# First group of sequences: value products ahead of the scores, f1 bias products behind them

## The chip, the cores and the metric

The kernel runs on one core of one Trainium2 chip. The metric is the device time of the program in microseconds (us); what is reported is the median of repeated runs.

## The reference, cut to what matters

One transformer layer in two halves, on x of 8 sequences x 512 tokens x 256 features, all in float32:

```
x = x + attn_block(layernorm(x))
x = x + ffn_block(layernorm(x))

attn_block(x):
  xn = layernorm(x, ln1_w, ln1_b)
  Q = elu(xn q_w' + q_b) + 1      # 64 features
  K = elu(xn k_w' + k_b) + 1
  V = xn v_w' + v_b               # 256 features
  out_n = sum_{m<=n} (Q_n.K_m) V_m / (sum_{m<=n} Q_n.K_m + 1e-6)
  x = x + out o_w' + o_b
  h = gelu(layernorm(x, ln2_w, ln2_b) f1_w' + f1_b)    # 1024
  return x + h f2_w' + f2_b

ffn_block(x):
  h = layernorm(gelu(x ternary(W_fc)'), ln_w, ln_b)    # 1024
  return h ternary(W_proj)'
```

`ternary(W)` rounds W / mean(|W|) to -1, 0 or 1.

## The kernel before

One sequence is one group g, 0 to 7. A group has four token tiles of 128. Each engine (TensorE: PE and its weight load PEld; VectorE: DVE; ScalarE: ACT; GpSimd: POOL; the DMA queue: SP) runs a list of steps in the order written in its functions `first()` (group 0 and the start of group 1), `step(g)` and `last()`. Nothing else sets the order: every step waits on semaphores, and whatever stands behind a waiting step on its engine waits with it. In `step(g)` the attention work of group g + 1 is mixed into the feed-forward work of group g, so TensorE always has something to run. Group 0's attention has no such partner: it is the prologue.

A float32 product of full accuracy is made as three products of split operands (`split3`, L177 to L179): hi by hi, lo by hi, hi by lo. ACT writes the hi half of an operand out of PSUM, DVE the lo half.

PSUM has eight banks: `bank_f0`, `bank_f1` (f1 and fc), `bank_y0`, `bank_y1` (f2, transposes of h), `bank_p` (projection), `bank_a0`, `bank_a1`, and `bank_a2`, which is also called `bank_q`.

The steps of the prologue, in TensorE's order before:

- `qkb`, `wvo_mm`, `tu(0, 0)`, `tu(0, 1)`, `qk_mm(0)`: bias of q and k, the product of the value and output weights, the transposes of u, and the products for Q and K into `bank_q`.
- `bvo` (L210): four products of 256 columns for the bias row, into `bank_p`.
- `f1b` (L218): 16 float32 products of **one column** each for the bias of f1, into `bank_y0`; every one needs a full weight load. The trace shows each as two records, 32 in all. DVE's `f1_bias_add` reads them; the first reader of its result is `gelu(0, 0)`.
- `scores(0)` (L271, L272): Q by K, eight products of 128 columns into `bank_q` (diagonal tiles), then 384, 384, 128, 128 columns into `bank_a0`, and 256, 256 into `bank_a1`. It waits for `qk_lo`, the last step of a chain through DVE and ACT that begins with `qk_mm(0)`. The three parts are masked and split by `ad_mask`, `ad_hi`, `ad_lo`, `ae_hi`, `ae_lo`, `af_hi`, `af_lo`.
- `v_mm(0, 0)`, `v_mm(0, 1)` (L177 to L179): 24 products of 256 columns, the values, into `bank_a0` and `bank_a1`. Those banks hold scores until `ae_lo` and `af_lo` have read them, so the values wait for these. ACT's `v_hi` and DVE's `v_lo` split the values.
- `attend(0, 0)` to `attend(0, 3)` (L303, then L177 to L179): for each token tile one product with the eps row (33 rows of weights) and 3, 6, 9 and 12 split products of 258 columns; 34 products in all. DVE's `attn_out` divides and adds.
- `tz2(0, 0)`, `theta_sum`, `tz2(0, 1)`, `f1(0, 0)` and so on: transposes of z, the mean of |W|, and the feed-forward products.

On the DMA queue (SP) the load of the projection weights, `pj_raw`, stands behind two waits, and the loads of x for group 1 behind it:

```
            sp.wait_ge(s["wf1_lo"], 4)
            sp.wait_ge(s["f1b_done"], 1)
            sp.dma_start(pj_raw, pj_d).then_inc(s["pj_loaded"], 16)
            load_x(1)
```

ACT's `abs_part(2)` and `abs_part(3)` read `pj_raw`, and stand on ACT ahead of `z2_norm(0, 0)`.

Of the kernel before, what the change touches and what calls it, by code (L numbers as in the profile page):

```python
# [8 lines left out]
ACT = mybir.ActivationFunctionType  # L9
AXX = mybir.AxisListType.X  # L10

P = 128
# [7 lines left out]
def build(nc, x, wqk_d, wv_d, wo_d, f1_d, f2_d, fc_d, pj_d, vec_d, rows_d, out):  # L20
    G, N, D = x.shape
# [13 lines left out]
    with ExitStack() as ctx:  # L35
# [11 lines left out]
        def by_k(b):  # L47

            return b[:].rearrange("p (k n) -> p k n", k=KD)

        wqk = [sb("wqk_hi", [P, KD, P], F32R), sb("wqk_lo", [P, KD, P], F32R)]
        wvo = [sb("wvo_hi", [P, KD, D], F32R), sb("wvo_lo", [P, KD, D], F32R)]
# [121 lines left out]
        def _(pe):  # L174
            def split3(ps, w, r, start, stop, skip=False):

                pe.matmul(ps, w[0], r[0], start=start, stop=False, skip_group_check=skip)  # L177
                pe.matmul(ps, w[0], r[1], start=False, stop=False, skip_group_check=skip)  # L178
                return pe.matmul(ps, w[1], r[0], start=False, stop=stop, skip_group_check=skip)  # L179
# [9 lines left out]
            def qkb():  # L189
                pe.wait_ge(s["wqk_loaded"], 16)  # L190
                pe.wait_ge(s["vec_loaded"], 16)
                for k in range(KD):
                    mm = pe.matmul(bank_f[0][:, 0:1], wqk_raw[:, k, :], ln1b_c[:, k:k + 1],
                                   start=(k == 0), stop=(k == KD - 1))
                mm.then_inc(s["qkb_done"], 1)

            def wvo_mm():
                pe.wait_ge(s["wv_loaded"], 16)
                pe.wait_ge(s["wo_loaded"], 16)
                for c in range(KD):  # L200
                    for k in range(KD):
                        mm = pe.matmul(bank_y[1][:, c * D:(c + 1) * D], wv_raw[:, k, c * P:(c + 1) * P],
                                       wo_raw[:, k, :], start=(k == 0), stop=(k == KD - 1))
                mm.then_inc(s["wvo_done"], 1)
# [74 lines left out]
                block_of(bank_a[1][:, 0:2 * P], 1, 2 * P, N).then_inc(s["s_done"], 1)  # L279

            def v_mm(g, h):
                pe.wait_ge(s["ae_lo" if h == 0 else "af_lo"], g + 1)
                if g == 0:
                    pe.wait_ge(s["wvo_lo"], 2)
                for j in range(2):
                    t = 2 * h + j
                    for k in range(KD):
                        mm = split3(bank_a[h][:, j * D:(j + 1) * D], [r[:, k, t * P:(t + 1) * P] for r in uT],
                                    [w[:, k, :] for w in wvo], k == 0, k == KD - 1)
                mm.then_inc(s["v_done"], 1)  # L290

            def attend(g, t):

                pe.wait_ge(s["v_lo"], 2 * g + t // 2 + 1)
                if t == 0:
                    pe.wait_ge(s["ad_lo"], g + 1)
                    if g == 0:
                        pe.wait_ge(s["eps_ready"], 1)
                        pe.wait_ge(s["rows_w"], 7)
                if t == 3:  # L300
                    pe.wait_ge(s["xa_ready"], 4 * g + 1)
                b = (bank_q, bank_a[0], bank_a[1], bank_q)[t]
                pe.matmul(b[:, 0:VW], ones_row[:], eps_row[:], start=True, stop=False)  # L303
                for j in range(t + 1):
                    if j == t:
                        w = [a[:, t * P:(t + 1) * P] for a in ad]
                    elif j == 1:
                        w = [a[:, (t - 2) * P:(t - 1) * P] for a in af]
                    else:
                        c = t - 1 if j == 0 else 3  # L310
                        w = [a[:, c * P:(c + 1) * P] for a in ae]
                    mm = split3(b[:, 0:VW], w, [r[:, j, :] for r in v], False, j == t)
                mm.then_inc(s["av_done"], 1)
# [85 lines left out]

            def first():  # L400

                qkb(); wvo_mm(); tu(0, 0); tu(0, 1); qk_mm(0); bvo(); f1b(); scores(0); v_mm(0, 0); v_mm(0, 1)
                attend(0, 0); attend(0, 1); attend(0, 2); attend(0, 3); tz2(0, 0); theta_sum(); tz2(0, 1); f1(0, 0)
                f1(0, 1); f1(0, 2); f1(0, 3); f2(0, 0); f2(0, 1); f2(0, 2); tu(1, 0); tu(1, 1); f1(0, 4); cpj()
                qk_mm(1); f2(0, 3); f1(0, 5); spread(); f1(0, 6); f2(0, 4); f2(0, 5); f1(0, 7); scores(1); f2(0, 6)
                f2(0, 7); v_mm(1, 0); v_mm(1, 1); attend(1, 0); attend(1, 1); tz3(0, 0); attend(1, 2); fc(0, 0, 0)
                tz3(0, 1); attend(1, 3); fc(0, 0, 1); fc(0, 1, 0); fc(0, 1, 1); tr(0, 0, 0); fc(0, 2, 0)
                tr(0, 0, 1); fc(0, 2, 1); tr(0, 0, 2); fc(0, 3, 0); proj(0, 0, 0); tr(0, 0, 3); tz2(1, 0)
                fc(0, 3, 1); proj(0, 0, 1); tz2(1, 1); tr(0, 1, 0); proj(0, 0, 2); proj(0, 0, 3)
# [35 lines left out]
        def _(act):  # L445
# [106 lines left out]
            def v_hi(g, h):  # L552
                act.wait_ge(s["v_done"], 2 * g + h + 1)
                if g:
                    act.wait_ge(s["av_done"], 4 * g)
                act.activation(v[0][:, 2 * h:2 * h + 2, 0:D], by_k(bank_a[h]), ACT.Copy).then_inc(s["v_hi"], 1)  # L556

            def z2_norm(g, h):
                act.wait_ge(s["ln2_sh"], 2 * g + h + 1)
# [53 lines left out]
            def first():  # L613

                ln3_hi(); wqk_hi(); u_norm(0, 0); u_norm(0, 1); u_hi(0, 0); u_hi(0, 1); wvo_hi(); qk_exp(0)
                wf1_hi(0); qk_hi(0); wf1_hi(1); n1(0); ae_hi(0); af_hi(0); wf1_hi(2); wf1_hi(3); ad_hi(0)
                v_hi(0, 0); eps_split(); v_hi(0, 1); abs_part(0); abs_part(1); abs_part(2); abs_part(3)
                z2_norm(0, 0); z2_norm(0, 1); z2_hi(0, 0); z2_hi(0, 1); gelu(0, 0); gelu(0, 1); gelu(0, 2)
                u_norm(1, 0); gelu(0, 3); u_norm(1, 1); u_hi(1, 0); u_hi(1, 1); gelu(0, 4); rows(); n1(1); qk_exp(1)
                gelu(0, 5); qk_hi(1); spread_copy(); gelu(0, 6); gelu(0, 7); ae_hi(1); ad_hi(1); af_hi(1)  # L620
                v_hi(1, 0); v_hi(1, 1); z3_norm(0, 0); z3_hi(0, 0); z3_norm(0, 1); z3_hi(0, 1); gelu3(0, 0, 0)
                gelu3(0, 0, 1); gelu3(0, 1, 0); gelu3(0, 1, 1); g_hi(0, 0, 0); gelu3(0, 2, 0); g_hi(0, 0, 1)
                gelu3(0, 2, 1); z2_norm(1, 0); g_hi(0, 0, 2); gelu3(0, 3, 0); z2_norm(1, 1); z2_hi(1, 0)
                g_hi(0, 0, 3); z2_hi(1, 1); g_hi(0, 1, 0); u_norm(2, 0); gelu3(0, 3, 1)
# [31 lines left out]
        def _(dve):  # L656
# [134 lines left out]
            def lo_part(dst, b, hi, ready):  # L791
                dve.tensor_tensor(dst, b, hi.bitcast(F32), ALU.subtract).then_inc(s[ready], 1)  # L792
# [40 lines left out]

            def v_lo(g, h):
                dve.wait_ge(s["v_hi"], 2 * g + h + 1)
                lo_part(v[1][:, 2 * h:2 * h + 2, 0:D], by_k(bank_a[h]), v[0][:, 2 * h:2 * h + 2, 0:D], "v_lo")

            def attn_out(g, t):

# [81 lines left out]
            def first():  # L921

                consts(); ln1_stats(0); wqk_lo(); qk_bias_add(); ln1_shift(0); u_lo(0, 0); u_lo(0, 1); wide_cols()
                wvo_lo(); qk_max(0); bo_rows(); ln3_lo(); qk_sum(0); wf1_lo(0); qk_lo(0); wf1_lo(1); ad_mask(0)
                ae_lo(0); af_lo(0); f1_bias_add(); wf1_lo(2); wf1_lo(3); ad_lo(0); v_lo(0, 0); eps_lo(); v_lo(0, 1)
                attn_out(0, 0); ln2_stats(0, 0); attn_out(0, 1); ln2_stats(0, 1); attn_out(0, 2); ln2_var(0, 0)
                ln2_stats(0, 2); attn_out(0, 3); ln2_stats(0, 3); ln2_var(0, 1); ln2_shift(0, 0); ln2_shift(0, 1)
                threshold(); z2_lo(0, 0); z2_lo(0, 1); ln1_stats(1); ternary(0); ln1_shift(1); ternary(1)
                ternary(2); selectors(); ternary(3); u_lo(1, 0); u_lo(1, 1); qk_max(1); qk_sum(1); qk_lo(1)
                ad_mask(1); ad_lo(1); ae_lo(1); af_lo(1); y_sum(0, 0); ln3_stats(0, 0); y_sum(0, 1); v_lo(1, 0)  # L930
                ln3_shift(0, 0); ln3_stats(0, 1); v_lo(1, 1); ln3_shift(0, 1); z3_lo(0, 0); attn_out(1, 0)
                ln2_stats(1, 0); attn_out(1, 1); ln2_stats(1, 1); z3_lo(0, 1); ln2_var(1, 0); attn_out(1, 2)
                ln2_stats(1, 2); ln4_stats(0, 0); ln2_shift(1, 0); attn_out(1, 3); ln2_stats(1, 3); g_lo(0, 0, 0)
                ln2_var(1, 1); g_lo(0, 0, 1); ln2_shift(1, 1); ln1_stats(2); g_lo(0, 0, 2); z2_lo(1, 0)
                g_lo(0, 0, 3); z2_lo(1, 1); ln1_shift(2); ln4_stats(0, 1); ln4_var(0, 0); g_lo(0, 1, 0)
# [181 lines left out]
```

## Time and profile before

| | |
|---|---|
| median of 3 runs | 541.44 us (540.43 to 543.45) |
| the profiled execution's own time | 542.56 us |
| its span, first to last instruction | 540.7 us |
| TensorE busy | 516.9 us, 96% of the span |
| VectorE, ScalarE, GpSimd busy | 336.3, 290.0, 128.6 us |
| mean granted clock of TensorE | 0.952 of 2.4 GHz |
| TensorE idle between 40.84 and 48.30 us | all but three short pieces |

The profile gives times from the start of the span. "Granted clock" is 1.00 where TensorE ran at 2.4 GHz and 0.50 where it ran at 1.2 GHz. A timeline row gives the start, the length, the engine, the line, the operation, the tile written and the tiles read, the shape, a count, and in brackets how long the engine had been idle and what ended that. The lengths of successive products overlap, so the time that a product takes in a row of products is read from the distance of two starts.

### The profile page before, as it was taken

The page shows a single profiled execution, that of the slowest core. Times are in us where ns is not written, and L with a number is a line of the kernel's source. Part 1 is how long each engine was busy: PE and PEld are TensorE (multiplying, and loading weights), DVE is VectorE, ACT ScalarE, POOL GpSimd, SP SyncE. Part 2 cuts the span into 40 slices and gives each one's busy share as a digit, 9 for nine tenths or more (in the row PEclk, how much of TensorE's full clock was granted, in tenths as well). Part 3 has the DMA queues.
Part 4 walks back from the last instruction along what each step waited for, and adds up shares of the span by engine and source line. Part 5 has one row for each costly group of instructions (what it writes and reads, how often), then busy time and mean ns, then how long its engine had stood idle before and what let it go on. Part 6 is the DMA issues. An engine that isn't in the chain of part 4 may idle for free.

```text
span 540.7 us, 8083 instructions
## 1 busy us (share of the span) xinstructions
PE 516.9 (96%) x2802; PEld 437.4 (81%) x2802; DVE 336.3 (62%) x930; ACT 290.0 (54%) x543; POOL 128.6 (24%) x128
## 2 busy tenths in 40 slices
PE   4895999999999999999999999999999999999887
PEld 3774878888888878888789888888788888888766
DVE  2668526865578627865388636776288725692467
ACT  3564652776248634677158553577248653563063
POOL 3204103422044021511144021420244102340110
PEclk9777998999999989999899998999899998999989
DMA  7130000100010000100000000100001000000001
GB/s 282 59 118 1 1 0 1 39 21 1 1 60 2 19 1 19 41 21 0 1 31 30 21 0 1 59 21 1 0 21 39 22 1 0 21 0 21 0 21 39
DMA packets 10039, 14.02 MB, mean 26 GB/s; under 512 B 784, under 2 KB 9104, under 8 KB 9488
## 3 DMA queue, kind: packets, MB, share of 16 engines
q1 hardware_dynamic: 10000, 13.52, 7.1%
q8 instruction: 22, 0.36, 0.3%
q14 instruction: 17, 0.14, 0.1%
HBM read 9.32 MB, written 4.19 MB: 25 GB/s over the span
## 4 chain that ended last, share of the span: by engine, by line
PE 92%; DVE 4%; ACT 1%; issue 1%; DMA 1%; SPq 0%; POOL 0%; DVEq 0%; ACTq 0%; POOLq 0%
PE bank_y L345 22%; PE bank_f L364 11%; PE bank_p L394 10%; PE bank_f L177 6%; PE bank_f L179 6%; PE bank_f L178 6%; PE bank_a L177 5%; PE bank_y L378 5%; PE bank_a L179 4%; PE bank_a L178 4%; PE bank_a L272 3%; PE bank_a L271 3%; PE bank_a L185 3%; PE bank_a L303 2%; PE bank_f L185 1%
## 5 line engine op out<-in xcount | busy, mean ns | idle before, releaser
L345 PE MATMUL bank_y<-wf,hring 128*128 128x256 f32 x512 | 121.5, 398 | 0.0
L345 PEld LDWEIGHTS bank_y<-wf,hring 128*128 128x128 f32 x512 | 103.4, 202 | 16.7 <-issue 0.2
L1003 POOL TENSOR_TENSOR rs<-ve,neg_half 128x2 f32<-128x2 f32 x48 | 33.6, 700 | 252.7 <-DVE ve L765 252.6
L909 DVE SCALAR_TENSOR_TENSOR g_lo<-bank_y,vec,g_hi 128x256 fp32r<-128x256 f32 x128 | 55.7, 477 | 23.4 <-ACT g_hi L610 22.6
L394 PE MATMUL bank_p<-wpj_t,g_hi 128*128 128x256 f32 x256 | 64.4, 288 | 0.5 <-DVE g_lo L909 0.5
L610 ACT ACTIVATE g_hi<-bank_y,vec 128x256 fp32r<-128x256 f32 x128 | 53.3, 472 | 20.8 <-PE bank_y L378 20.7
L579 ACT ACTIVATE hring<-bank_f,f_bias 128x512 f32<-128x512 f32 x64 | 43.9, 687 | 37.1 <-PE bank_f L179 36.3
L394 PE MATMUL bank_p<-wpj_t,g_lo 128*128 128x256 f32 x256 | 62.0, 279 | 0.0
L177 PE MATMUL bank_f<-z2T_hi,wf_hi 128*128 128x512 f32 x128 | 54.9, 429 | 1.4 <-DVE z2T_lo L792 1.4
L364 PE MATMUL bank_f<-wfc_t,z3T_hi 128*128 128x512 f32 x128 | 54.2, 423 | 0.5 <-DVE z3T_lo L792 0.5
L179 PE MATMUL bank_f<-z2T_hi,wf_lo 128*128 128x512 f32 x128 | 52.7, 411 | 0.0
L178 PE MATMUL bank_f<-z2T_lo,wf_hi 128*128 128x512 f32 x128 | 52.5, 410 | 0.0
L601 ACT ACTIVATE h<-bank_f 128x512 f32<-128x512 f32 x64 | 38.0, 596 | 25.2 <-PE bank_f L364 23.7
L364 PE MATMUL bank_f<-wfc_t,z3T_lo 128*128 128x512 f32 x128 | 51.1, 400 | 0.0
L394 PEld LDWEIGHTS bank_p<-wpj_t,g_hi 128*128 128x128 f32 x256 | 48.1, 188 | 1.5 <-DVE g_lo L909 0.7
L1021 POOL TENSOR_TENSOR xa<-xa,bo_b 128x512 f32<-128x512 f32 x16 | 20.4, 1293 | 119.1 <-ACT xa L498 119.1
L394 PEld LDWEIGHTS bank_p<-wpj_t,g_lo 128*128 128x128 f32 x256 | 48.2, 188 | 0.5
L889 DVE BATCH_NORM_STATS2 bn<-h 128x6 f32<-128x512 f32 x64 | 41.7, 682 | 4.2 <-ACT h L601 4.0
L378 PE MATMUL bank_y<-ident,h 128*128 128x128 f32 x256 | 37.0, 272 | 0.0
L378 PEld LDWEIGHTS bank_y<-ident,h 128*128 128x128 f32 x256 | 30.5, 141 | 3.7
L556 ACT ACTIVATE v_hi<-bank_a 128x512 fp32r<-128x512 f32 x16 | 9.6, 600 | 42.4 <-PE bank_a L179 42.4
L498 ACT ACTIVATE z<-y,sh,rs 128x256 f32<-128x256 f32 x32 | 17.5, 594 | 26.4 <-DVE sh L770 26.4
(155 smaller groups left out, 1015.1 us busy)
## 6 DMA issues: line engine op xcount, KB each, us to landing
x_sb<-in_x SPq DMA_DIRECT2D x16, 256.0 KB, 2.8
out<-yc SPq DMA_DIRECT2D x16, 256.0 KB, 2.1
h<-in_f SPq DMA_DIRECT2D x1, 1024.0 KB, 7.8
wf<-in_f SPq DMA_DIRECT2D x1, 1024.0 KB, 9.7
h<-in_fc SPq DMA_DIRECT2D x1, 1024.0 KB, 11.7
h<-in_pj SPq DMA_DIRECT2D x1, 1024.0 KB, 4.8
hring<-in_wv SPq DMA_DIRECT2D x1, 256.0 KB, 3.9
hring<-in_wo SPq DMA_DIRECT2D x1, 256.0 KB, 4.8
```

The costliest lines, as they stand in the source:

```text
L177: pe.matmul(ps, w[0], r[0], start=start, stop=False, skip_group_check=skip)
L178: pe.matmul(ps, w[0], r[1], start=False, stop=False, skip_group_check=skip)
L179: return pe.matmul(ps, w[1], r[0], start=False, stop=stop, skip_group_check=skip)
L345: mm = pe.matmul(bank_y[t // 2][:, (t % 2) * D:(t % 2 + 1) * D], hring[:, (8 * g + k) % RH, t * P:(t + 1) * P], wf2[:, k, :], start=(k == ...
L364: mm = pe.matmul(bank_f[c][:], z3T[part][:, k, t * P:(t + 1) * P], wfc[:, k, c * 512:(c + 1) * 512], start=(k == 0 and part == 0), stop=(k ...
L378: mm = pe.transpose(bank_y[q % 2][:, (2 * i + t) * P:(2 * i + t + 1) * P], h3[:, 2 * h + t, m * P:(m + 1) * P], ident[:])
L394: mm = pe.matmul(bank_p[:, t * D:(t + 1) * D], gr[part][:, (8 * g + 4 * h + q) % RG, i, t * P:(t + 1) * P], wpj[:, m, :], start=(m == 0 an ...
L579: act.activation(hring[:, (8 * g + m) % RH, :], bank_f[m % 2][:], ACT.Gelu, bias=f1_bias[:, m:m + 1]).then_inc(s["h_ready"], 1)
L601: act.activation(h3[:, t, c * 512:(c + 1) * 512], bank_f[c][:], ACT.Gelu).then_inc(s["h3_ready"], 1)
L610: act.activation(gr[0][:, n % RG, i, :], bank_y[q % 2][:, i * D:(i + 1) * D], ACT.Copy, scale=ln3w_c[:, m:m + 1]).then_inc(s["g_hi"], 1)
L889: dve.bn_stats(bn[3][:, t, 6 * c:6 * c + 6], h3[:, t, c * 512:(c + 1) * 512]).then_inc(s["ln4_bn"], 1)
L909: dve.scalar_tensor_tensor(gr[1][:, n % RG, i, :], bank_y[q % 2][:, i * D:(i + 1) * D], ln3w_c[:, m:m + 1], gr[0][:, n % RG, i, :].bitcast ...
```

## The change

In the first group only, the value products go to `bank_f0` and `bank_f1`, which are free then, so they no longer wait for the split of the scores; they wait for `wvo_lo` and for `qk_bias_ready` (the one-column product in `bank_f0` has been read). On TensorE they stand ahead of `scores(0)`, and `f1b` stands behind it. The waits for `ae_lo` and `af_lo` go to `attend(0, 1)` and `attend(0, 2)`, which write the banks that held the scores. ACT and DVE get the steps in a matching order: `v_hi`, `v_lo` right behind the split of q and k, `eps_split` and `eps_lo` ahead of the scores' split, `f1_bias_add` last. No instruction is added or removed.

```diff
+        def v_bank(g, h):
+
+            return bank_a[h] if g else bank_f[h]
...
             def v_mm(g, h):
-                pe.wait_ge(s["ae_lo" if h == 0 else "af_lo"], g + 1)
-                if g == 0:
+                if g:
+                    pe.wait_ge(s["ae_lo" if h == 0 else "af_lo"], g + 1)
+                else:
                     pe.wait_ge(s["wvo_lo"], 2)
+                    pe.wait_ge(s["qk_bias_ready"], 1)
...
+                if g == 0 and t in (1, 2):
+                    pe.wait_ge(s[("ae_lo", "af_lo")[t - 1]], 1)
...
-                qkb(); wvo_mm(); tu(0, 0); tu(0, 1); qk_mm(0); bvo(); f1b(); scores(0); v_mm(0, 0); v_mm(0, 1)
+                qkb(); wvo_mm(); tu(0, 0); tu(0, 1); qk_mm(0); bvo(); v_mm(0, 0); v_mm(0, 1); scores(0); f1b()
...
-                wf1_hi(0); qk_hi(0); wf1_hi(1); n1(0); ae_hi(0); af_hi(0); wf1_hi(2); wf1_hi(3); ad_hi(0)
-                v_hi(0, 0); eps_split(); v_hi(0, 1); abs_part(0); abs_part(1); abs_part(2); abs_part(3)
+                wf1_hi(0); qk_hi(0); v_hi(0, 0); v_hi(0, 1); n1(0); eps_split(); wf1_hi(1); ad_hi(0)
+                ae_hi(0); af_hi(0); wf1_hi(2); wf1_hi(3); abs_part(0); abs_part(1); abs_part(2); abs_part(3)
...
-                wvo_lo(); qk_max(0); bo_rows(); ln3_lo(); qk_sum(0); wf1_lo(0); qk_lo(0); wf1_lo(1); ad_mask(0)
-                ae_lo(0); af_lo(0); f1_bias_add(); wf1_lo(2); wf1_lo(3); ad_lo(0); v_lo(0, 0); eps_lo(); v_lo(0, 1)
+                wvo_lo(); qk_max(0); bo_rows(); ln3_lo(); qk_sum(0); wf1_lo(0); qk_lo(0); v_lo(0, 0); v_lo(0, 1); eps_lo(); ad_mask(0)
+                wf1_lo(1); ad_lo(0); ae_lo(0); af_lo(0); wf1_lo(2); wf1_lo(3); f1_bias_add()
```

`v_hi` and `v_lo` read `v_bank(g, h)` in place of `bank_a[h]`.

TensorE before, from the bias row's products to the first attend: first the f1 bias (reads `h3`, where the f1 weights lie), then the scores (`q_stack`, `k_stack`, `k_lo`), then the values (`wvo`, `uT`), then the eps row's product of `attend(0, 0)`.

```order
L210 MATMUL bank_p<-hring 128x256 [waits wvo_copied,wide_ready]
...
L218 MATMUL bank_y0<-vec,h3 128x1 [waits vec_loaded,f1_loaded]
L218 MATMUL bank_y0<-vec,h3 128x1 x15
L271 MATMUL bank_a2<-q_stack,k_stack 128x128 [waits qk_lo]
...
L272 MATMUL bank_a1<-q_stack,k_lo 128x256
L177 MATMUL bank_a0<-wvo_hi,uT_hi 128x256 [waits wvo_lo,ae_lo]
...
L177 MATMUL bank_a1<-wvo_hi,uT_hi 128x256 [waits wvo_lo,af_lo]
...
L303 MATMUL bank_a2<-eps_row,ones_row 128x258 [waits eps_ready,rows_w,ad_lo,v_lo]
```

The same stretch of TensorE now (the lines count 4 to 8 higher):

```order
L214 MATMUL bank_p<-hring 128x256 [waits wvo_copied,wide_ready]
...
L181 MATMUL bank_f0<-wvo_hi,uT_hi 128x256 [waits qk_bias_ready,wvo_lo]
...
L181 MATMUL bank_f1<-wvo_hi,uT_hi 128x256 [waits qk_bias_ready,wvo_lo]
...
L275 MATMUL bank_a2<-q_stack,k_stack 128x128 [waits qk_lo]
...
L276 MATMUL bank_a1<-q_stack,k_lo 128x256
L222 MATMUL bank_y0<-vec,h3 128x1 [waits vec_loaded,f1_loaded]
L222 MATMUL bank_y0<-vec,h3 128x1 x15
L311 MATMUL bank_a2<-eps_row,ones_row 128x258 [waits eps_ready,rows_w,ad_lo,v_lo]
```

The one-column products have moved from ahead of the scores to between the scores and the first attend, and the value products into their old place.

ScalarE before, from the split of q and k to the sums of |W| (the last of which wait for the load of the projection weights):

```order
L532 ACTIVATE k_stack<-bank_a2 64x512
L473 ACTIVATE wf1_hi<-h3,vec 128x512 [waits vec_loaded,f1_loaded]
L498 ACTIVATE xa<-x_sb,sh0,rs0 128x256 [waits ln1_sh]
...
L538 ACTIVATE ad_hi<-bank_a2 128x512 [waits ad_masked]
L556 ACTIVATE v_hi<-bank_a0 128x2x256 [waits v_done]
L465 ACTIVATE eps_row<-eps_raw 1x258 [waits rows_w,eps_raw_ready]
L466 ACTIVATE eps_hi<-eps_raw 1x258
L556 ACTIVATE v_hi<-bank_a1 128x2x256 [waits v_done]
L481 ACTIVATE yc,abs_sum<-h3 128x1024 [waits fc_loaded]
...
L481 ACTIVATE yc,abs_sum<-h3 128x1024 [waits abs_summed,pj_loaded] x2
L498 ACTIVATE z<-xa,sh1,rs1 128x256 [waits ln2_sh]
```

The same stretch of ScalarE now:

```order
L540 ACTIVATE k_stack<-bank_a2 64x512
L564 ACTIVATE v_hi<-bank_f0 128x2x256 [waits v_done]
L564 ACTIVATE v_hi<-bank_f1 128x2x256 [waits v_done]
L506 ACTIVATE xa<-x_sb,sh0,rs0 128x256 [waits ln1_sh]
...
L474 ACTIVATE eps_hi<-eps_raw 1x258
L481 ACTIVATE wf1_hi<-h3,vec 128x512 [waits vec_loaded,f1_loaded]
L546 ACTIVATE ad_hi<-bank_a2 128x512 [waits ad_masked]
...
L489 ACTIVATE yc,abs_sum<-h3 128x1024 [waits fc_loaded]
...
L489 ACTIVATE yc,abs_sum<-h3 128x1024 [waits abs_summed,pj_loaded] x2
L506 ACTIVATE z<-xa,sh1,rs1 128x256 [waits ln2_sh]
```

The split of the values has moved ahead of the normalising of x, and nothing stands between the scores' split and the sums of |W| any more.

## Rows read from the trace of the kernel before

**Rows 1.** The page: busy time of TensorE, and the chain that ended last, by engine.

```profile
PE 516.9 (96%) x2802; PEld 437.4 (81%) x2802; DVE 336.3 (62%) x930; ACT 290.0 (54%) x543; POOL 128.6 (24%) x128
...
PE 92%; DVE 4%; ACT 1%; issue 1%; DMA 1%; SPq 0%; POOL 0%; DVEq 0%; ACTq 0%; POOLq 0%
```

**Rows 2.** Timeline of TensorE: f1 bias, scores and values of group 0.

```profile
18.29 4.51 PE L218 MATMUL bank_y<-vec,h 128*128 128x1 f32 x32
23.36 0.48 PE L271 MATMUL bank_a<-q_stack,k_stack 128*128 128x128 f32 x1 [0.56 <-DVE k_lo L792]
...
28.63 0.58 PE L271 MATMUL bank_a<-q_stack,k_stack 128*128 128x256 f32 x1
29.14 0.58 PE L272 MATMUL bank_a<-q_stack,k_lo 64*128 64x256 f32 x1
30.11 0.58 PE L177 MATMUL bank_a<-wvo_hi,uT_hi 128*128 128x256 f32 x1 [0.39 <-DVE ae_lo L792]
30.49 0.42 PE L178 MATMUL bank_a<-wvo_lo,uT_hi 128*128 128x256 f32 x1
30.71 0.41 PE L179 MATMUL bank_a<-wvo_hi,uT_lo 128*128 128x256 f32 x1
```

**Rows 3.** The same timeline: attends of group 0, and f1's first product.

```profile
35.12 0.36 PE L303 MATMUL bank_a<-eps_row,ones_row 33*128 33x258 f32 x1
35.42 0.39 PE L177 MATMUL bank_a<-v_hi,ad_hi 128*128 128x258 f32 x1
35.64 0.28 PE L178 MATMUL bank_a<-v_lo,ad_hi 128*128 128x258 f32 x1
35.76 0.28 PE L179 MATMUL bank_a<-v_hi,ad_lo 128*128 128x258 f32 x1
35.97 0.38 PE L303 MATMUL bank_a<-eps_row,ones_row 33*128 33x258 f32 x1
...
40.55 0.29 PE L179 MATMUL bank_a<-v_hi,ad_lo 128*128 128x258 f32 x1
...
48.30 0.79 PE L177 MATMUL bank_f<-z2T_hi,wf_hi 128*128 128x512 f32 x1 [1.41 <-DVE z2T_lo L792]
```

**Rows 4.** Stretches: start:end, length, busy and count by engine, clock, DMA, GB/s.

```profile
20.00:21.00 1.00, 1.00 (x11) 1.00 (x10) 0.66 (x2) 0.94 (x2) 0.00 (x0) 0.91 0.00 0
22.80:23.36 0.56, 0.00 (x1) 0.00 (x1) 0.53 (x2) 0.56 (x2) 0.00 (x0) 0.50 0.00 0
30.11:34.40 4.29, 4.29 (x20) 4.29 (x21) 3.20 (x6) 3.03 (x7) 0.00 (x0) 0.50 0.24 59
48.30:51.50 3.20, 3.20 (x8) 2.52 (x9) 3.10 (x13) 0.76 (x2) 1.11 (x1) 0.50 0.01 3
75.83:78.80 2.97, 2.97 (x13) 1.89 (x11) 0.70 (x1) 0.69 (x1) 0.00 (x0) 1.00 0.00 0
80.11:85.60 5.49, 5.49 (x14) 4.41 (x14) 1.62 (x3) 0.49 (x2) 0.00 (x0) 0.50 0.00 0
135.28:139.28 4.00, 4.00 (x17) 2.56 (x15) 1.64 (x4) 0.60 (x1) 0.04 (x1) 1.00 0.01 2
```

**Rows 5.** Line L218 on TensorE, at 18 to 20.8 us and at 21.2 to 23 us.

```profile
L218 PE MATMUL bank_y<-vec,h x24: 167/250/317, 18.3 to 20.8; 128*128 128x1 f32 x24
L218 PE MATMUL bank_y<-vec,h x8: 352/352/353, 21.0 to 22.4; 128*128 128x1 f32 x8
```

**Rows 6.** DMA issues from 30 to 45 us: KB each, us to landing.

```profile
h<-in_pj SPq DMA_DIRECT2D x1, 1024.0 KB, 4.8
```

**Rows 7.** Timeline of ScalarE: last sums of |W|, first normalising of z.

```profile
38.32 1.06 ACT L481 ACTIVATE yc<-h 128x1024 f32<-128x1024 f32 x1
...
39.56 1.06 ACT L481 ACTIVATE yc<-h 128x1024 f32<-128x1024 f32 x1
...
42.66 1.09 ACT L498 ACTIVATE z<-xa,sh,rs 128x256 f32<-128x256 f32 x2 [1.95 <-DVE sh L770]
```

More of the change, by code:

```diff
@@ L287, in v_mm @@
                     for k in range(KD):
-                        mm = split3(bank_a[h][:, j * D:(j + 1) * D], [r[:, k, t * P:(t + 1) * P] for r in uT],
+                        mm = split3(v_bank(g, h)[:, j * D:(j + 1) * D], [r[:, k, t * P:(t + 1) * P] for r in uT],
                                     [w[:, k, :] for w in wvo], k == 0, k == KD - 1)
@@ L555, in v_hi @@
                     act.wait_ge(s["av_done"], 4 * g)
-                act.activation(v[0][:, 2 * h:2 * h + 2, 0:D], by_k(bank_a[h]), ACT.Copy).then_inc(s["v_hi"], 1)
+                act.activation(v[0][:, 2 * h:2 * h + 2, 0:D], by_k(v_bank(g, h)), ACT.Copy).then_inc(s["v_hi"], 1)
             def z2_norm(g, h):
@@ L835, in v_lo @@
                 dve.wait_ge(s["v_hi"], 2 * g + h + 1)
-                lo_part(v[1][:, 2 * h:2 * h + 2, 0:D], by_k(bank_a[h]), v[0][:, 2 * h:2 * h + 2, 0:D], "v_lo")
+                lo_part(v[1][:, 2 * h:2 * h + 2, 0:D], by_k(v_bank(g, h)), v[0][:, 2 * h:2 * h + 2, 0:D], "v_lo")
             def attn_out(g, t):
```

## The prediction

> **What bounds the kernel now.** I read the page first: TensorE is busy for 96% of the span, and the chain that ended last runs through it for 92% [rows 1]. So a microsecond counts in two cases only: TensorE's own work gets longer, or its start in the prologue is put off. After f1 of group 0 has begun at 48.30 us [rows 3] TensorE hardly stops again, and nothing that this change touches lies behind that point. The whole question is therefore when that product starts. The timeline of TensorE gives the prologue: the f1 bias from 18.29 us, the scores from 23.36, when DVE's `k_lo` is ready, the values from 30.11, when `ae_lo` is ready [rows 2], the attends from 35.12 to 40.84 (last start 40.55 plus 0.29), then a tail of 7.46 us through DVE, POOL, ACT and four transposes to 48.30 [rows 3]. The reader is to see in it that f1 starts 7.46 us after the last attend, whatever comes before, and that TensorE idles only 0.56 + 0.39 us between the bias row and the attends [rows 2].
>
> The stretches give the second thing to see: the granted clock. It is at its upper level (2.4 GHz) while the f1 bias starts and falls during it, in the last fifth of the stretch 20 to 21 us; it stays at the lower level (1.2 GHz) through the gap and the scores, and is still there at 34.40, when the values have run without a gap for 4.3 us [rows 4]. The attends run at the upper level: their successive products start 0.12 us apart against 0.22 for the values [rows 3, 2].
>
> **The change part by part.**
>
> *The values* (24 products) take the place of the f1 bias, behind the bias row's products at 18.29 us, in front of the scores. The clock is at the upper level there, so they cost 24 x 0.12 = 2.9 us and end near 21.2; at the lower level 24 x 0.21 = 5.1, and they end at 23.4. Either is covered by the wait for `k_lo`, which ends at 23.36 and which no moved step of ACT or DVE precedes. The scores therefore start at 23.36 as before. What the values cost behind the scores, 35.12 - 30.11 = 5.0 us, and the wait of 0.39 us for `ae_lo`, are gone from the path.
>
> *The scores* ran from 23.36 to 29.65 (29.14 plus the distance of 0.51), 6.3 us, at the lower clock. All at the upper level they take 4.0 us, as group 2 shows (135.28 to 139.28, clock 1.00 [rows 4]). The clock is now at the upper level when they start. In group 1 it was at the upper level for 3.0 us of scores, falling just behind 78.8, although TensorE had come to them without a gap [rows 4]. Here it has been idle for 2.1 us before, so I let 0.9 us of scores be fast, which is 0.9 x (6.3 / 4.0 - 1) = 0.5 us gained; bounds 0 and 2.3. The scores end at 29.15.
>
> *The f1 bias* now lies between them and the first attend. It has 32 passes. While the clock was at the upper level 24 of them started within 2.5 us, 0.107 apart; behind 21 us the distance is (22.4 - 21.0) / 7 = 0.20 to 0.21 [rows 5]. At 29 us the clock is at the lower level in the trace of before, under the same scores, and nothing in the change would lift it by then. So 32 x 0.21 = 6.7 us, and with the last pass's own length and the switch to the eps row (0.2) the first attend starts at 36.1 instead of 35.12: **+1.0 us**. The bounds: 32 x 0.107 = 3.4 us (attends at 32.8, -2.3 us) and, without the 0.5 us on the scores, 36.6 (+1.5). I take 6.7, since eight passes were measured at that level and the scores kept it there.
>
> Nobody needs this result so early: the first reader of the f1 bias is the gelu behind 48.30. Its place makes the attends wait for it all the same.
>
> *The attends* lose what warmed the clock for them: 5 us of values without a gap. Now they follow 7 us of one-column products, during which the clock fell when it was up. Their price at the lower level, by the nearest rows: a plain product 0.215 against 0.12 us (22 distances, +2.05); the eps product, which switches to weights of another height, 0.51 as the scores' 256-column products (28.63 to 29.14) against 0.30 (4 times, +0.84); the first product behind it 0.38 as at 30.11 to 30.49, against 0.22 (4 times, +0.64); the product ahead of an eps row the same 0.38 against 0.21 (3 times, +0.50); the last one's length 0.41 against 0.29 (+0.12) [rows 2, 3]. Sum **+4.15 us**: 9.9 in place of 5.7 us. When would the clock rise? It had not yet risen after 4.3 us of values (it rose 4.4 us in), not after 3.2 us of f1 (soon behind that) and not after 5.5 us of f2 behind the scores of group 1 [rows 4], and all these ran without a gap. In the attends the columns fill 34 x 0.215 = 7.3 of 9.9 us, with gaps at each of the four eps rows. The bounds are a rise 3.2 us in (3.2 + 0.68 x 5.72 = 7.1 us, +1.4) and none (+4.15). I take none, because the work that has such gaps, the scores, never lifted the clock, and all that lifted it had none.
>
> *ACT and DVE* only have earlier work earlier. The eps row is ready near 26.3 (four normalisings of x, then the two copies, then one subtraction), the scores' splits near 30, all covered by the f1 bias. If that cover were gone they would be ready 4 to 5 us before 35.12 in any case.
>
> *The queue.* The load of the projection weights waits for `f1b_done`, so it leaves at 36.2 instead of 32.2, with the loads of x behind it, and lands 4.8 us later [rows 6], at 41.0. Two sums of |W| follow, 1.24 us each [rows 7]: 43.5. Behind them ACT has to normalise z, 1.8 us after the last attend (42.66 against 40.84 [rows 7, 3]), which will be at 46.0 + 1.8 = 47.8. So 4 us of cover; if the attends were fast, (36.1 + 5.7 + 1.8 = 43.6) it would just be used up. x of group 1 lands near 42 and is first read behind 51.
>
> *The sum*: +1.0 + 4.15 = +5.1 us at the end of the attends, and the tail of 7.46 us carries it to f1 and to the end. Against the profiled execution's own 542.56 that is 547.7; this execution lies 1.1 us above the median of its three runs, 541.44, so the median of the new kernel should be **546.5 us**.
>
> **The page on weight loads.** The rows show the distance of one-column passes doubling with the clock, 0.107 to about 0.21 us [rows 5]. The Trainium skill, page "TensorE: Matmul & The Clock Gate", section "LDWEIGHTS (loading the stationary operand)", gives the time of a weight load as its columns over 1.2, with no term for the clock's level. By that rule the 32 passes would not stretch.
>
> **The rivals.**
>
> A. *The clock rises within the attends*, 4.4 us in, as it did for the values: 4.4 + (1 - 4.4 / 9.9) x 5.72 = 7.6 us, +1.9. With +1.0 that is +2.9: 544.3. For it: the attends are the densest work since the values. Against it: their gaps.
>
> B. *Faster, because the clock holds.* If the clock outlives the scores, as it did in group 2 [rows 4], the scores end at 27.4, the f1 bias takes 3.4 us, the attends run from 31.0 to 36.7: -4.1 us, 537.3. It decides at one point, the level at about 29 us. Against it: 2.1 us of idle time and then thin work, where in the trace the one-column products alone made it fall. A smaller form of it, where the clock comes back before the f1 bias ends, has no row for it.
>
> C. *The weight loads keep their time at the lower clock* (32 x 0.107 = 3.4 us), the attends are slow: 32.8 + 9.9 = 42.7 against 40.84, +1.9, 543.3. The eight passes at 0.20 to 0.21 speak against it. This is what the skill's rule would do here.
>
> D. *The load of the projection weights becomes the last thing*: if it takes 9 us in place of 4.8, the normalising of z waits until 47.7, still no later than forecast. So it costs nothing beside slow attends; it decides only where the attends are fast, and then brings A up by at most 1 us. It is no case of its own.
>
> E. *f1 also starts colder.* It ran 3.2 us at the lower level, the shortest of the three rises. With 4.4 or 5.5 us the same f1 costs up to 2.3 / 2 = 1.1 us more: 547.6. This can fall either way in both kernels.
>
> **How the numbers follow.** Forecast with E in its range, 545 to 548: 0.60. A, 543.5 to 545: 0.22. C: 0.05. B: 0.05. That something unseen hides or undoes the whole, within 1.5 us of before: 0.08. A range from 543.0 to 548.3 leaves out B, the last case and a little of each end. A measurement of this kernel can tell about 0.5%, 2.7 us, from no change: slower is above 544.1, which is the forecast and half of A and some scatter, 0.71; within is the rest of A, C, the unseen case and the weaker part of B, 0.25; faster 0.04.
>
> **What would show it right or wrong.** In the profile of the changed kernel: values from about 18.3 to 21.2 us at clock 1.00; scores from 23.4, clock falling within 1 us or so; the f1 bias from about 29.2 with passes 0.21 us apart; the first attend near 36.1 at clock 0.50, plain products 0.215 apart, the last ending near 46; f1 near 53.4. Wrong would be a clock of 1.00 during the f1 bias, attends that turn fast in their middle (A), passes of 0.107 us at clock 0.50 (C), or a normalising of z that waits for the sums of |W| (D).

## The result, and the profile after

The changed kernel is **slower by 0.65%**: 544.43 us (median of 20 runs, 542.55 to 548.56) against 541.17 us (20 runs, 538.06 to 543.81); ratio 1.0065, 95% interval 1.0043 to 1.0087. That is +3.3 us, in the interval 2.3 to 4.7. Forecast were 546.5 us and +5.1. The measured time lies inside the stated range of 543.0 to 548.3, but in the part of it that the forecast gave to rival A (543.5 to 545, chance 0.22), not in its own 545 to 548.

The profiled execution took 544.61 us, its span 542.8. The page of the changed kernel, busy time and chain by engine, answers to [rows 1]:

```profile
PE 518.0 (95%) x2802; PEld 439.0 (81%) x2802; DVE 336.2 (62%) x930; ACT 289.9 (53%) x543; POOL 128.4 (24%) x128
...
PE 92%; DVE 4%; ACT 1%; DMA 1%; issue 1%; SPq 0%; POOL 0%; DVEq 0%; ACTq 0%; POOLq 0%
```

Nothing there shows where 3 us went; the prologue does. Timeline of TensorE in the changed kernel, which answers to [rows 2, 3]:

```profile
16.43 1.89 PE L214 MATMUL bank_p<-hring 128*128 128x256 f32 x8
17.97 0.47 PE L181 MATMUL bank_f<-wvo_hi,uT_hi 128*128 128x256 f32 x1
...
20.89 0.28 PE L183 MATMUL bank_f<-wvo_hi,uT_lo 128*128 128x256 f32 x1
23.24 0.33 PE L275 MATMUL bank_a<-q_stack,k_stack 128*128 128x128 f32 x1 [2.07 <-DVE k_lo L800]
...
27.34 0.58 PE L276 MATMUL bank_a<-q_stack,k_lo 64*128 64x256 f32 x1
27.85 6.99 PE L222 MATMUL bank_y<-vec,h 128*128 128x1 f32 x32
34.76 0.58 PE L311 MATMUL bank_a<-eps_row,ones_row 33*128 33x258 f32 x1
...
43.65 0.28 PE L183 MATMUL bank_a<-v_hi,ad_lo 128*128 128x258 f32 x1
...
51.40 0.79 PE L181 MATMUL bank_f<-z2T_hi,wf_hi 128*128 128x512 f32 x1 [1.41 <-DVE z2T_lo L800]
```

The reader is to see four lengths. The values take 3.2 us and hide in the wait for `k_lo`. The scores take 4.6 us, from 23.24 to 27.85, against 6.3 before. The f1 bias takes 6.9 us. The attends take 43.93 - 34.76 = **9.2 us against 5.7**. They start 0.36 us *earlier* than before and end 3.1 later; f1 starts 7.47 us behind them, as before.

The clock in the same stretches (columns as in [rows 4]): values, the first 2.7 us of the scores, f1 bias, attends up to 42.9, the rest of the attends, and f1's first products.

```profile
18.00:21.00 3.00, 3.00 (x26) 2.93 (x24) 2.17 (x6) 1.78 (x4) 0.00 (x0) 1.00 0.00 0
23.24:25.90 2.66, 2.66 (x10) 1.84 (x10) 1.58 (x3) 2.61 (x7) 1.93 (x2) 1.00 0.00 0
27.85:34.60 6.75, 6.75 (x33) 6.75 (x32) 3.27 (x6) 4.43 (x9) 0.00 (x0) 0.50 0.00 0
34.76:42.90 8.14, 8.14 (x29) 6.56 (x29) 3.69 (x14) 2.30 (x4) 0.55 (x1) 0.50 0.56 194
43.00:43.90 0.90, 0.90 (x8) 0.72 (x6) 0.00 (x0) 0.00 (x0) 0.06 (x1) 0.97 0.00 0
51.40:56.60 5.20, 5.20 (x12) 4.13 (x13) 4.84 (x17) 1.21 (x2) 2.08 (x1) 0.50 0.00 0
```

The clock falls 2.8 us into the scores, stays at the lower level through the whole f1 bias, and comes back only 8.2 us into the attends, when six products are left.

**A ruler for the comparisons.** The origin of a profile moves by up to 1.8 us with the first loads, so I count from the start of the bias row's products (L210, here L214, at 16.56 before and 16.43 after) to the start of f1. It is **31.74 us before and 34.97 after: +3.23**, as much as the medians differ (+3.3). The two spans differ by 2.1 only, because the clock also falls in the scores of later groups, at other points and for other lengths in the two profiles. Group 1's first product of 384 columns lies 61.20 us behind the ruler's start before and 65.38 after (+4.2, f1 having run colder by 1.0), group 2's 120.84 and 123.47 (+2.6), group 3's 180.89 and 185.11 (+4.2), group 7's 428.58 and 431.08 (+2.5). So the ruler shows what the change does to the prologue; that it agrees with the medians to 0.1 us is partly luck.

### The profile page after: what moved, and what is told of

It reads as the page before. It is cut to its first block, busy times and chain, and to the rows that moved or that the text cites. A ratio compares the mean times of both kernels' runs of the same rounds, so it can differ in the third digit from the quotient of the medians.

```text
span 542.8 us, 8085 instructions
## 1 busy us (share of the span) xinstructions
PE 518.0 (95%) x2802; PEld 439.0 (81%) x2802; DVE 336.2 (62%) x930; ACT 289.9 (53%) x543; POOL 128.4 (24%) x128
## 4 chain that ended last, share of the span: by engine, by line
PE 92%; DVE 4%; ACT 1%; DMA 1%; issue 1%; SPq 0%; POOL 0%; DVEq 0%; ACTq 0%; POOLq 0%
PE bank_y L353 21%; PE bank_f L372 11%; PE bank_p L402 10%; PE bank_f L181 6%; PE bank_f L182 6%; PE bank_f L183 6%; PE bank_y L386 5%; PE bank_a L181 5%; PE bank_a L183 4%; PE bank_a L182 4%; PE bank_a L276 3%; PE bank_a L275 3%; PE bank_a L189 3%; PE bank_a L311 2%; PE bank_y L222 1%; PE bank_f L189 1%
## 5 line engine op out<-in xcount | busy, mean ns | idle before, releaser
L353 PE MATMUL bank_y<-wf,hring 128*128 128x256 f32 x512 | 118.0, 390 | 0.0
L353 PEld LDWEIGHTS bank_y<-wf,hring 128*128 128x128 f32 x512 | 101.0, 198 | 15.8 <-issue 0.2
L618 ACT ACTIVATE g_hi<-bank_y,vec 128x256 fp32r<-128x256 f32 x128 | 53.4, 473 | 20.8 <-PE bank_y L386 20.7
L181 PE MATMUL bank_f<-z2T_hi,wf_hi 128*128 128x512 f32 x128 | 56.3, 440 | 1.4 <-DVE z2T_lo L800 1.4
L182 PE MATMUL bank_f<-z2T_lo,wf_hi 128*128 128x512 f32 x128 | 53.8, 420 | 0.0
L181 PEld LDWEIGHTS bank_f<-z2T_hi,wf_hi 128*128 128x128 f32 x128 | 25.8, 202 | 7.5 <-DVE z2T_lo L800 1.8
```

The source lines that it names most:

```text
L353: mm = pe.matmul(bank_y[t // 2][:, (t % 2) * D:(t % 2 + 1) * D], hring[:, (8 * g + k) % RH, t * P:(t + 1) * P], wf2[:, k, :], start=(k == ...
L618: act.activation(gr[0][:, n % RG, i, :], bank_y[q % 2][:, i * D:(i + 1) * D], ACT.Copy, scale=ln3w_c[:, m:m + 1]).then_inc(s["g_hi"], 1)
```

## The experiments

The theory: the one-column products stand on the path and leave the clock low for the attends. The rivals: something in ACT's, DVE's or the queue's order; the banks; the f1 bias as the only thing that holds the clock down. In the diffs below only the core is shown. The ruler and the length of the attends come from one profile each; the next column is the time of that profiled execution itself. Behind it stand the median and the ratio to the kernel before, which was measured anew beside each kernel (medians 541.16 to 541.56 us):

| kernel | ruler, us | attends, us | profiled execution, us | median, us | ratio (95%) |
|---|---|---|---|---|---|
| before | 31.74 | 5.7 | 542.56 | 541.17 | |
| changed | 34.97 | 9.2 | 544.61 | 544.43 | 1.0065 (1.0043, 1.0087) |
| changed, second profile | 34.96 | 9.1 | 543.46 | 543.46 (1 run) | |
| 14 of 16 bias products left out | 29.81 | 9.7 | 540.45 | 539.02 | 0.9975 (0.9955, 0.9995) |
| f1 bias ahead of the values | 33.95 | 8.3 | 543.82 | 540.30 | 1.0004 (0.9978, 1.0029) |
| banks only | 31.26 | 5.7 | 541.09 | 540.89 | 1.0001 (0.9980, 1.0023) |
| 64 columns each | 35.06 | 9.4 | 543.78 | 543.98 | 1.0056 (1.0032, 1.0080) |
| 128 columns each | 30.80 | 5.7 | 537.88 | 541.42 | 0.9998 (0.9972, 1.0024) |
| before, 128 columns each | 30.17 | 5.7 | 542.90 | 540.83 | 0.9999 (0.9982, 1.0015) |
| split | 30.39 | 9.6 | 539.65 | 539.38 | 0.9962 (0.9948, 0.9977) |
| split, larger part ahead of values | 29.79 | 8.1 | 538.51 | 540.04 | 0.9977 (0.9959, 0.9995) |
| split, larger part between them | 31.62 | 9.3 | 541.67 | 541.03 | 0.9990 (0.9969, 1.0011) |
| split, reordered | 29.53 | 8.9 | 538.70 | 537.67 | 0.9933 (0.9909, 0.9957) |
| split, reordered, 128 columns | 27.51 | 8.6 | 536.69 | 537.64 | 0.9932 (0.9908, 0.9957) |

### Without the f1 bias products

```diff
-                for m in range(KH):
+                for m in range(1):
```

> The changed kernel with 14 of the 16 one-column products of the f1 bias left out (every column of the bias takes the value of the first). This measures what these products cost where they now stand. Theory 1 (they lie on the path, and the attends behind them run at the lower clock for their own sake): scores 23.2 to 27.9 us as in the changed kernel, first attend when the scores are split, near 29, attends 8 to 9.5 us long, last attend ends near 38, f1 starts near 45.5, the time is about 6 us below the changed kernel and 2.7 below the kernel before: 538.5. Rival (the f1 bias itself is what keeps the clock low, and the attends would be fast behind the scores): attends 5.7 us, last one ends near 35, f1 near 42.5, time 535.5.

Measured 539.02 us. The attends start 12.6 us behind the ruler's start in place of 18.3, and are slow all the same. Timeline and clock of this kernel:

```profile
27.34 0.58 PE L311 MATMUL bank_a<-eps_row,ones_row 33*128 33x258 f32 x1
```

```profile
27.34:36.90 9.56, 9.56 (x35) 7.86 (x34) 5.59 (x18) 5.54 (x10) 0.71 (x1) 0.50 0.47 167
37.00:38.00 1.00, 0.08 (x1) 0.00 (x0) 0.81 (x3) 0.00 (x0) 0.00 (x0) 0.70 0.00 0
```

Two things follow. The products cost 5.2 us of prologue where they stand (34.97 - 29.81): the attends start 5.7 us earlier without them (28 passes left out at 0.215 are 6.0, and the scores came out 0.2 to 0.3 slower), and take about 0.5 longer. And they are not what makes the attends slow: with only two bias products left between them and the scores, these run 9.6 us at the lower clock. The rival that blamed the f1 bias alone fell. What the attends miss, compared with the kernel before, is the work of the values right in front of them.

### The f1 bias back in its place, values ahead of the scores

```diff
-                ... bvo(); v_mm(0, 0); v_mm(0, 1); scores(0); f1b()
+                ... bvo(); f1b(); v_mm(0, 0); v_mm(0, 1); scores(0)
```

> The changed kernel with one thing undone: the f1 bias products stand behind the bias row's again, ahead of the values; the order is f1 bias, values, scores, attends. Theory 1 (place of the f1 bias decides): the f1 bias runs 18.0 to 22, the values behind it at the lower clock to about 27, so the scores start 3.5 us late, near 27, and end near 32 to 33; attends at once behind them. If the values lift the clock, scores and attends are partly fast and the last attend ends near 40.5; if not, near 42. Time 541 to 543. Rival (the change's loss has another cause, in the order of ACT or DVE): it stays at the changed kernel's 544.4.

Measured 540.30, below the 541 to 543 expected and within 0.3% of the kernel before. ACT and DVE keep the changed order here, and the loss of 3.3 us is gone, so that rival fell. (A small cost of their order that the earlier values make up for is not excluded by this run; the kernel with 128 columns below, which also keeps their order, leaves no room for a large one.) The profiled execution is not typical: it took 543.82 us, while seven of the 12 executions took 539.6 to 540.3. It shows the clock falling 2.2 us into the f1 bias, the scores starting 11.3 us behind the ruler's start in place of 6.8, and a wait that I had not named:

```profile
34.15 0.55 PE L311 MATMUL bank_a<-eps_row,ones_row 33*128 33x258 f32 x1 [2.50 <-DVE ad_lo L800]
```

When nothing lies between scores and attends, the split of the scores is in the way.

### The banks alone

```diff
-                pe.wait_ge(s["ae_lo" if h == 0 else "af_lo"], g + 1)
+                if g:
+                    pe.wait_ge(s["ae_lo" if h == 0 else "af_lo"], g + 1)
...
-                        mm = split3(bank_a[h][:, j * D:(j + 1) * D], ...
+                        mm = split3(v_bank(g, h)[:, j * D:(j + 1) * D], ...
```

> The kernel before with one part of the change alone: the values of the first group go to the two banks of f1, and their waits for the split of the scores move to the attends; no step is moved. Theory 1 (the banks only take away the wait of 0.39 us behind the scores, the order did the rest): the values start 0.3 to 0.4 us earlier, everything else as before, time 541.2 - 0.4 = 540.8, same as before. Rival (the banks themselves cost something): 542 or more.

Measured 540.89. The ruler is 0.48 us shorter, about the wait of 0.39 that went; the medians can't tell it from nothing. The banks cost nothing that shows; the loss is in the order.

### Fuller passes, 64 and 128 columns

```diff
-                        mm = pe.matmul(bank_y[0][:, m:m + 1], f1_raw[:, k, m * P:(m + 1) * P], ln2b_c[:, k:k + 1],
+                        mm = pe.matmul(bank_y[m // 4][:, (m % 4) * 128:(m % 4 + 1) * 128], f1_raw[:, k, m * P:(m + 1) * P],
+                                       ln2b_c[:, k:k + 1].to_broadcast([P, 128]),
```

With 64 columns all results fit one bank. With 128 they take two, so DVE adds the bias in two steps, and the waits that belong to these banks and steps are adapted.

> The changed kernel, where each one-column product of the f1 bias streams 64 equal columns (the same column repeated) into 64 columns of the bank, of which one is read: same number of weight loads, same place, same result. Tells whether it is the emptiness of these products that keeps the clock low. Theory 1 (the weight loads set the distance of the passes and the streamed columns lift the clock): passes 0.21 us apart as before until the clock rises within the f1 bias or soon after it, attends at 1.00 for the most part and 5.7 to 7 us long, last attend ends 39.5 to 41.5, time 540 to 542. Rival (half-filled passes lift nothing): same stretch as in the changed kernel, clock 0.50 until 43, 544.4. A third way: wider passes take longer than 0.21 us each, and the first attend starts later than 34.8.

> The changed kernel, where each product of the f1 bias streams 128 equal columns in place of one, into two banks; same weight loads, same place, same result. With 64 columns nothing was lifted and the passes stayed 0.215 us apart. Theory 1a (what lifts the clock is how full the passes are; with 128 columns the engine streams all the time): the clock rises within the f1 bias, about 4.5 us in, the f1 bias takes 5 to 6 us, the attends run at 1.00 and take 5.7 us; from the start of the bias row's products to f1's start 30.3 us (31.74 in the kernel before, 34.97 in the changed one), time 539.5 to 540.5. Rival (it is the kind of product, float32 with a weight load for each, that lifts nothing): 35 us, 544. Third (128 columns lengthen the passes): the first attend starts later than 18.3 us behind the bias row's products.

With 64 columns nothing moved (543.98, ruler 35.06): the rival held, these passes lifted nothing. With 128 columns the clock rose within the f1 bias, 5.5 us in, and the attends ran at the upper level. Clock of this kernel in the f1 bias, at its end, and in the attends:

```profile
26.79:32.20 5.41, 5.41 (x26) 5.41 (x26) 3.45 (x6) 4.61 (x9) 0.00 (x0) 0.50 0.00 0
32.00:33.00 1.00, 1.00 (x10) 1.00 (x8) 0.00 (x0) 0.00 (x0) 0.00 (x0) 0.85 0.00 0
33.17:38.80 5.63, 5.63 (x35) 4.59 (x34) 3.76 (x15) 0.65 (x1) 0.66 (x1) 1.00 0.73 266
```

This is the run that settles it: the same TensorE instructions in number and order, the same place, the same weight loads, only more columns streamed, and the attends take 5.7 us instead of 9.2. The ruler gives back 4.2 us: 3.5 in the attends, 0.5 in the f1 bias (6.4 us instead of 6.9, where 5 to 6 were expected), 0.2 in the scores. The median gives back 3.0 (541.42; 539.5 to 540.5 was expected, so that part missed). The loss of the change in the prologue is the clock in the attends; their start had come no later than before. The profiled execution took 537.88 us, 3.5 less than the median, but that doesn't come from the prologue: from group 3's first product of 384 columns to group 4's it took 60.06 us, against 63.10 in the profile of the kernel before. The passes had hardly lengthened, 5.1 us for 23 distances, 0.22:

```profile
L223 PE MATMUL bank_y<-vec,h x24: 421/421/581, 26.8 to 31.9; 128*128 128x128 f32 x24
```

### The f1 bias in gaps of TensorE

```diff
+                ... tu(0, 1); f1b(range(2)); qk_mm(0); bvo(); v_mm(0, 0); v_mm(0, 1); f1b(range(2, KH)); scores(0)
```

> The changed kernel with the f1 bias products put into gaps of TensorE ahead of the scores: 4 of the 16 between the transposes of u and the products for Q and K (TensorE waits there from 13.6 to 15.0 us), 12 between the values and the scores (a wait of 2.1 us). Theory 1: both are covered but for 0.3 us or so, the scores start at 23.3 to 23.8, the clock falls earlier in them, they end near 29.5, and the attends follow at once, slow, to about 39: f1 near 46.5, time 1.5 to 2 us below the kernel before, 539.5, and 5 below the changed one. Rival (slow attends eat it all): at or above the kernel before, 541 or more.

Measured 539.38, 0.4% below the kernel before, as the theory had it. The 24 passes between values and scores run at the upper clock in 2.6 us, where 24 distances of 0.215 behind the scores are 5.2, and the attends start 13.3 us behind the ruler's start instead of 18.3. They are slow throughout:

```profile
20.16:22.80 2.64, 2.64 (x27) 2.64 (x25) 1.81 (x3) 2.59 (x6) 0.00 (x0) 0.98 0.02 6
22.90:28.90 6.00, 6.00 (x15) 3.94 (x15) 4.09 (x7) 3.69 (x8) 2.49 (x2) 0.50 0.00 0
28.92:38.40 9.48, 9.48 (x35) 7.70 (x34) 5.78 (x18) 5.72 (x10) 0.71 (x1) 0.50 0.49 167
```

Two other places for the larger part, `bvo(); f1b(range(2, KH)); v_mm(0, 0); v_mm(0, 1); scores(0)` and `v_mm(0, 0); f1b(range(2, KH)); v_mm(0, 1); scores(0)`:

> The f1 bias in two parts as in the split kernel, but the larger part between the bias row's products and the values, so that the full products of the values stand right in front of the scores. Theory 1: where the clock holds through 2.6 us of one-column products, the values end at 23.6 us, scores start at once and run faster than in the split kernel (5 us in place of 6.1), 1 us better, 538.4; where it falls within them, the values take up to 5.1 us, the scores start up to 2.5 us late, 541. In all 539 to 541, and more scatter than the split kernel (539.4).

> The same, with the larger part of the f1 bias between the first and the second half of the values. Theory 1: between the other two, 538.5 to 540.5; the two halves of the values keep the clock up more surely than in one piece ahead of or behind the f1 bias, so less scatter.

540.04, within the 539 to 541 expected, and 541.03, above the 538.5 to 540.5 expected. Neither beat 539.38, though the first can't be told from it (the intervals overlap). In the first the scores were fast throughout (3.8 us), as hoped, but the attends then waited 3.04 us for `ad_lo`, which took most of that gain: they started 14.2 us behind the ruler's start instead of 13.3. They were 1.5 us shorter, so the ruler still came out 0.6 below the split kernel's; this profile is of the shortest of 12 executions, 538.51. In the second, meant to hold the clock more surely, it fell all the same within the second half of the values, and the scores started 7.9 us behind the ruler's start, against 7.2 in the split kernel. That expectation missed.

### Split, with ACT and DVE reordered, and with full passes

```diff
-                ... v_hi(0, 1); n1(0); eps_split(); wf1_hi(1); ad_hi(0)
-                ae_hi(0); af_hi(0); wf1_hi(2); ...
+                ... v_hi(0, 1); eps_split(); n1(0); ad_hi(0)
+                ae_hi(0); af_hi(0); wf1_hi(1); wf1_hi(2); ...
                 ... ad_mask(0)
-                wf1_lo(1); ad_lo(0); ...
+                ad_lo(0); ae_lo(0); af_lo(0); wf1_lo(1); ...
```

> The split kernel (f1 bias in two parts, both ahead of the scores) with ACT's and DVE's steps around the scores in another order: the split of the eps row ahead of the normalising of x, and the f1 weights' second quarter behind the split of the scores. Theory 1: where the scores end early, the attends wait for ad_lo (3.0 us in the kernel with the larger part ahead of the values, 0 to 0.5 in the split one), so this gains 0 to 0.5 us here: 539.0. Rival: x of group 0 is normalised later and DVE's attn_out waits for it, 0.5 us lost: 540.

> The same with 128 equal columns streamed by each product of the f1 bias. Theory 1a (full passes hold the clock up): the clock does not fall in the 2.6 us of the second part, nor in the first 3 us of scores, the scores take 4.3 to 5 us in place of 6.1, ad_lo is ready when they end, attends from 26.7 to 28 us (counted as in the kernel before), slow as long as nothing full precedes them: 1 to 2 us better than without the wide columns, 537.5. Rival (the scores' end is not what counts, since slow attends take 9.6 us whenever they start and the clock's return moves with them): 539.

537.67 and 537.64: **both are faster than either kernel, by 0.67% and 0.68% against before.** The first gained 1.7 us on the split kernel where at most 0.5 was expected. It has six executions only, three at 536.5 to 536.8 and three at 538.5 to 538.8, so its median falls between the two and is less sure than the others. Its profile starts the attends 13.2 us behind the ruler's start, 0.2 better; the rest of its 0.9 us on the ruler is a clock that rose within the attends, and what makes up the remainder is not settled. In the second the clock held through the f1 bias and the scores (3.9 us), the attends started 11.5 us behind the ruler's start, and the ruler is 2.0 us shorter; the median shows none of it. Its number, 537.5, was expected from a gain of 1 to 2 us on a kernel at 539, and neither part came, so that hit is luck. The clock did in the prologue what the theory says, and the gain doesn't show in the median. In the two profiles the lead of 2.0 us at f1 is still 1.7 us at group 7's first product of 384 columns, and 0.8 us at the end.

### The kernel before with full passes

> The kernel before, with only the 128 equal columns streamed by each product of the f1 bias. Theory 1a: the clock, which fell at 20.8 within the f1 bias, holds through it and through the first 3 us of scores; the scores end 1.5 to 2 us earlier, and the values with the attends behind them start as much earlier: 539.5. Where the values are then run at the lower clock for longer, part is given back. Rival (the fall at 20.8 only moves into the wait of 1.9 us for k_lo, which is then longer): as the kernel before, 541.

Measured 540.83, where 539.5 was expected: the clock held through the f1 bias and 3 us of scores, and the ruler became 1.6 us shorter, but the median moved by no more than its scatter. It is the rival's number, 541, without the rival's mechanism, since the scores did end earlier. By the positions of the first product of 384 columns the gain is still there in group 7 (427.40 us behind the ruler's start against 428.58), and the last 98.0 us take 2.4 us more than the 95.6 before. The clock in a stretch of that last part, before and then in this kernel:

```profile
504.00:524.00 20.00, 15.73 (x82) 13.04 (x81) 11.08 (x30) 7.28 (x15) 3.89 (x4) 0.91 0.04 14
```

```profile
503.20:523.20 20.00, 15.72 (x76) 12.95 (x75) 10.74 (x29) 6.94 (x14) 3.90 (x4) 0.83 0.04 14
```

The clock was low for longer in this stretch, with the same work. But it is one execution, at 542.90 us the longest of this kernel's 12. Over all 14 profiles that last part takes 94.9 to 97.1 us in the eleven without full bias passes, and 96.2, 96.2 and 98.0 in the three with them. No run was made to tell chance from rule here; this stays open, for the wide kernels too.

### A second profile of the changed kernel

> The changed kernel once more, for a second profile: where the clock rises and falls. If the clock follows what the engine has done and not the place in the program alone, the fall in the scores and the rise in the attends lie up to 3 us from 26.0 and 43.0 us, and the start of f1, counted from the bias row's products, differs from 34.97 us by up to 1.5 us.

Little scatter showed, far less than the bounds of the expectation allowed: the clock fell 2.6 us into the scores and rose 8.1 us into the attends (2.8 and 8.2 in the first), and the ruler read 34.96 against 34.97. How the longest executions ran (up to 548.56 us) is not shown.

## Why the prediction was right, and where its sizes were off

- **What bounds the kernel: right.** The time followed the start of f1: +3.23 us on the ruler, +3.3 in the medians. The tail of 7.46 us [rows 3] came out as 7.47, and as 7.46 to 7.48 in every kernel run here.
- **The values: right.** 17.97 to 21.17, hidden, clock 1.00; scores at 23.24.
- **The scores: mis-sized.** The step "I let 0.9 us of scores be fast" gave 0.5 us; 2.8 us were fast and the gain was 1.7 (6.3 less 4.6), inside its bounds of 0 and 2.3. The reason that I gave, that 2 us of idle time ahead would bring the fall forward, didn't hold: the clock fell as far into the scores as in group 1 [rows 4], where there was no gap. This accounts for 1.2 of the 1.8 us between the forecast of +5.1 and the measured +3.3, and is most of why the first attend came 0.36 us early and not 1.0 late.
- **The f1 bias: right.** 32 passes 0.215 us apart, 6.9 us with the switch. Rival C fell: for these float32 passes the distance doubles with the lower clock, 0.107 us [rows 5] against 0.215. The Trainium skill, page "TensorE: Matmul & The Clock Gate", section "LDWEIGHTS (loading the stationary operand)", gives a weight load a time without a term for the clock; an estimate by it for 32 loads of 128 columns is 3.4 us. The measurement decides.
- **The attends: right in kind, 0.7 us too long.** +3.45 us in place of +4.15. The distances at the lower clock were as priced: eps product 0.51, first product 0.38, plain 0.215. What was off is "none" for the rise: it came 8.2 us in. Rival A, with 4.4 us, was further off. That the work in front decides, as forecast, is shown by the kernel with 128 columns. The forecast named two things, the values gone and the one-column products in their place; the kernel with 14 of the 16 left out shows that the first is enough for slow attends.
- **The queue: as forecast.** Load issued at 34.93, landed 5.0 us later, and two sums of |W| behind it; ACT's wait for it was covered by 3.5 us, since z had to wait for DVE anyway (compare [rows 6, 7]):

```profile
39.92 1.06 ACT L489 ACTIVATE yc<-h 128x1024 f32<-128x1024 f32 x1 [7.56 <-DMA h<-in_pj]
...
45.76 1.09 ACT L506 ACTIVATE z<-xa,sh,rs 128x256 f32<-128x256 f32 x2 [3.45 <-DVE sh L778]
```

- **E, f1 starts colder: it did**, 5.3 us at the lower level against 3.2, worth 1.0 us at group 1. By group 2 more than that was given back (+2.6 in place of +4.2), and at group 3 it stood at +4.2 again.
- **B, the clock holds: fell** in the form written, since it was at the lower level at 29 us.
- **What was luck.** Both mis-sized terms, 1.2 us in the scores and 0.7 in the attends, erred the same way, and the stated range held their sum. Rival A's 544.3 us lies closer to the measured 544.43 than the forecast does, but for no good reason: it adds a first attend 1.0 us late (it came 0.36 early) and attends 1.9 us longer (3.45).

## What to carry to other kernels

Before thin products are moved in front of a dense chain, ask what the chain loses in front of it: here 5 us of values had been paying for the clock of the 34 products that followed, and "hiding" them in a wait cost the attends 3.5 us. A pass of one column took here as long as one of 64 or 128 (0.215 to 0.22 us at the lower clock), and one of a single column half of that at the upper one (0.107 [rows 5]); put such products where the clock is still up and the engine waits anyway (24 passes in 2.6 us here, against 5.2 at the lower clock), not between a result and its reader. And count the gain in the median of many runs, not at the point that was mended: 1.6 and 2.0 us won in the prologue did not show in the medians.

## What the runs showed of the hardware

- Passes of 1 or 64 columns behind a weight load, 0.215 us apart without a gap, left the clock at the lower level for 7 us; in passes of 128 columns at 0.22 it rose after 5.5 us. A busy TensorE in the profile does not say that the clock will rise.
- In attends that began at the lower level, 34 products with gaps at four eps rows, the clock rose 8.2 us in once, 8.1 in the second profile, and not at all in 9.6 us in the kernel with 14 of the 16 bias products left out.
- A subtraction of one row on DVE (the eps row) took 1.17 us while POOL's addition on 128 x 512 ran, and 0.42 us before, without POOL beside it. It is so in all 14 profiles: 1.15 to 1.17 us in the nine where it starts within POOL's addition, 0.42 in the five where it does not. Why was not tested. From the timeline of DVE and of POOL in the changed kernel:

```profile
25.58 1.17 DVE L709 TENSOR_TENSOR eps_row<-eps_raw,eps_hi 1x258 fp32r<-1x258 f32 x1 [1.08 <-ACT eps_hi L474]
```

```profile
23.97 2.50 POOL L1029 TENSOR_TENSOR xa<-xa,bo_b 128x512 f32<-128x512 f32 x2 [11.57 <-ACT xa L506]
```
